# Attention score matmuls of one decoder layer: two heads of 64 rows side by side in three passes, in place of one head of 128 stacked rows in two

## The chip, the core and the metric

The kernel runs on one core of one Trainium2 chip. A core has five engines that run their own instruction lists and meet only through semaphores: TensorE (PE in the profile; its weight loads have a row of their own, PEld), VectorE (DVE), ScalarE (ACT), GpSimd (POOL) and SyncE (SP), which here only starts DMAs. Matmul results land in PSUM (8 banks of 128 partitions by 512 fp32 numbers); everything else lives in SBUF, also 128 partitions. The metric is device time of one execution in microseconds (us).

## The reference

One decoder layer over x of shape (4, 512, 512): an attention block with memory slots, a cross attention, a gated FFN, each followed by a residual sum and a layer norm. The change touches the first block alone. For each batch b and each of 16 heads (64 query/key columns, 64 slots, 128 value columns) that block computes

```
q, k, v, g, s = x@Wq, x@Wk, x@Wv, x@Wg, clip(x@Ws, -32, 32)
z  = cumlogsumexp(s, time)            # running normaliser of the slots
hk = hk * exp(z[t-1] - z[t]) + k[t] (outer) exp(s[t] - z[t])
pv = softmax(q[t] @ hk)               # 64 slots
hv = hv * exp(z[t-1] - z[t]) + exp(s[t] - z[t]) (outer) v[t]
o[t] = pv @ hv
out = (rmsnorm(o) * gnorm * silu(g)) @ Wo
```

The two recurrences are computed as causal attention: with E = exp(s) and 1/Z its running sum, the first is causal(q k^T) @ E / Z, the second causal((softmax / Z) E^T) @ v. So each step needs two score products of the same form: a 64-row "left" operand (k, later E) against a 64-row "right" operand (q, later w = pv/Z), 512 by 512 with the lower half left out.

## The kernel before

**Precision.** TensorE takes fp32r operands in one pass, which keeps only the high part of an fp32 number. Each operand is therefore split into `hi` (the fp32r rounding, a cast on ACT) and `lo` (what is left, a subtraction on DVE), and a product is hi·hi + hi·lo + lo·hi. `mm3` (L61 to L66) issues the three passes for projections with 128 contraction rows.

**Scores before.** A head's score has only 64 contraction rows, half of the 128 of the array. `left[:, h]` therefore stacks the hi half and the lo half of the left operand of head h over 128 partitions, and `right_hi[:, h]`, `right_lo[:, h]` hold the right operand twice, on both halves. One pass with `right_hi` gives hi·hi + lo·hi, one with `right_lo` gives hi·lo + lo·lo: two passes (L469, L471) a head and key block.

**Work of a step.** The attention block is 32 steps (8 pairs of heads by 4 batches), numbered n. The first pair and the last are unrolled, the six between run as a hardware loop of 4 steps. Two heads of one pair share each step: their projected operands lie on partitions 0 to 63 and 64 to 127, as the projections leave them in PSUM (`HALF`). PE's order in a step is written by hand (`step`, L525):

1. `chunks(n, 0)`: scores of k and q; then the S projection of the next step
2. `slots`: causal scores times E, L499, 64 output partitions a head; then transposes, projections and the output projection of the step before
3. `chunks(n, 1)`: scores of E and w; then the Q and K projections of the next step
4. transposes of E, then `values` (L515)

**One call of `chunks`** goes through three chunks c: key block 0 (512 columns, banks `ch[0]`, `ch[1]` for the two heads), key block 1 (384 columns, banks `okb`, `tb`), key blocks 3 and 2 (256 columns each, banks `ch` again). Since c = 2 writes the banks that c = 0 wrote, PE waits ahead of c = 2 on `chunk_act`: ACT must have copied chunk 0 out (`copy_chunk0`, L618), one copy a head. DVE copies and masks chunks 1 and 2 (L729), POOL masks the diagonal blocks of chunk 0 (L356) after ACT's copy. `slots` and `values` wait on all of these. There are 64 calls in all.

**ACT and DVE around it.** `high_right`/`low_right` and `high_left`/`low_left` prepare the operands: 4 and 4 instructions of 64 partitions for a right operand, 2 and 2 for a left one. Each step prepares two of each: E's left after the first call, w's right before the second call, the next step's q and k after it. ACT's list in a step starts with `copy_chunk0(n, 0)`, right behind the squares (L662) of the step before; POOL's list starts with the mask of chunk 0, right behind `factor` (L363 to L371), a chain of five small operations on the sums of those squares.

Of the kernel before, what the change touches and what calls it, by code (L numbers as in the profile page):

```python
# [125 lines left out]
def phase_attention(nc, x, Wq, Wk, Wv, Wg, Ws, Wo, gw, acc, ident, norm):  # L126
# [5 lines left out]
    with ExitStack() as ctx:  # L132
# [18 lines left out]
        left = sb("left", [P, 2, T], F32R)  # L151
        right_hi = sb("right_hi", [P, 2, T], F32R)
        right_lo = sb("right_lo", [P, 2, T], F32R)
# [263 lines left out]
        def _(pe):  # L417
# [12 lines left out]
            def project(m, i, b, pair):  # L430
# [3 lines left out]
                if i == S:  # L434
                    wait(pe, right_ready, 2 * m)
                    pe.wait_ge(s_ready, pair + 1)
                elif i == VG:
                    wait(pe, left_ready, 2 * m)
# [18 lines left out]
            def chunks(n, which):  # L457

                for c in range(3):
                    for h in range(2):  # L460
                        bank = (okb, tb)[h] if c == 1 else ch[h]

                        if c == 0:
                            wait(pe, chunk_dve, 8 * n + 4 * which - 1 + h)
                        elif c == 2:
                            pe.wait_ge(chunk_act, 4 * n + 2 * which + h + 1)
                        for i, col, first in CHUNKS[c]:
                            out = bank[:, col:col + T - first]
                            pe.matmul(out, left[:, h, i * P:(i + 1) * P], right_hi[:, h, first:T],  # L469
                                      start=True, stop=False)  # L470
                            mm = pe.matmul(out, left[:, h, i * P:(i + 1) * P], right_lo[:, h, first:T],  # L471
                                           start=False, stop=True)
                        mm.then_inc(chunk_done, 1)
# [51 lines left out]
            def step(n, p, j, first, last):  # L525
# [7 lines left out]
                pe.wait_ge(left_ready, 2 * (2 * n) + 2)  # L533
                pe.wait_ge(right_ready, 2 * (2 * n) + 2)
# [18 lines left out]
                pe.wait_ge(left_ready, 2 * (2 * n) + 4)  # L553
                pe.wait_ge(right_ready, 2 * (2 * n) + 4)
# [28 lines left out]
        def _(act):  # L583
# [5 lines left out]
            def high_left(src):  # L589
                for h in range(2):  # L590
                    nc.scalar.copy(left[HALF[h], h, :], src[HALF[h], :]).then_inc(left_hi_ready, 1)
# [39 lines left out]
            def step(n, p, j, first, last):  # L631
# [8 lines left out]
                act.wait_ge(chunk_done, 12 * n + 6)  # L640
                high_left(eT)
# [13 lines left out]
                act.wait_ge(chunk_done, 12 * n + 12)  # L655
# [22 lines left out]
        def _(dve):  # L678
# [7 lines left out]
            def low_left(src, turn):  # L686
                for h in range(2):
                    dve.wait_ge(left_hi_ready, 2 * turn + h + 1)
                    nc.vector.tensor_tensor(left[HALF[1 - h], h, :], src[HALF[h], :],
                                            left[HALF[h], h, :].bitcast(F32), ALU.subtract).then_inc(left_ready, 1)  # L690

            def low_right(src, turn):
                for h in range(2):
# [1037 lines left out]
```

## Time and profile before

| what | value |
|---|---|
| time, median of 3 runs | 2264.56 us (2264.44 to 2269.01) |
| profiled execution, first to last instruction (span) | 2263.2 us |
| mean granted TensorE clock | 0.981 |
| PE busy / PEld busy | 2153.7 us / 1632.5 us |
| DVE / ACT / POOL busy | 1565.8 / 989.7 / 550.8 us |
| last instruction of `values` in the attention block | begins at 1318.7 us |

The profile gives the span of its own execution and not what lies around it. The median stands 1.4 us above that span. A matmul in the trace is shown from its start to its modelled end, which overlaps the next one, so what one costs the stream is the distance between starts. Where "[0.26 <-POOL ...]" stands behind a row, the engine had shown nothing for that long, and the name says what ended it.

### The profile page before, as it was taken

How to read it: one execution, taken by the hardware profiler on the slowest of the kernel's cores; microseconds unless marked ns; L12 is line 12 of the kernel's file. 1: busy time of each engine (PE TensorE's matmuls, PEld its weight loads, DVE VectorE, ACT ScalarE, POOL GpSimd, SP SyncE). 2: the span in 40 equal slices, each digit the busy share in tenths (PEclk: the TensorE clock that was granted, in tenths of full speed). 3: DMA queues.
4: the chain of work that ended last, by engine and by line, in shares of the span. 5: the costliest groups of instructions: out<-in, count | busy, mean ns of one | idle time of the engine just before them, and what ended most of it. 6: DMA issues, size and time to landing. Idle time of an engine off the chain costs nothing. (4 is left out here: it accounts for less than half of the span.)

```text
span 2263.2 us, 32522 instructions
## 1 busy us (share of the span) xinstructions
PE 2153.7 (95%) x11316; PEld 1632.5 (72%) x11316; DVE 1565.8 (69%) x2455; ACT 989.7 (44%) x2026; POOL 550.8 (24%) x632
## 2 busy tenths in 40 slices
PE   7999999999999999999999968999999979999996
PEld 6788878888787888878888754555555458778784
DVE  4776767767677676767768868888888645455557
ACT  2443443434344443444434324777777742111211
POOL 3142251232243142232422231221211011111111
PEclk9999999999999999999999978999999989999998
DMA  4000100101001001001000000000000010000001
GB/s 149 1 1 10 33 10 1 33 10 34 1 10 34 1 11 33 1 10 33 1 10 1 1 10 7 14 14 14 14 13 8 2 28 28 15 28 14 28 14 74
DMA packets 56039, 42.60 MB, mean 19 GB/s; under 512 B 13936, under 2 KB 46704, under 8 KB 55920
## 3 DMA queue, kind: packets, MB, share of 16 engines
q1 hardware_dynamic: 55920, 40.92, 5.9%
q8 instruction: 87, 1.43, 0.3%
q14 instruction: 32, 0.26, 0.0%
HBM read 32.78 MB, written 4.19 MB: 16 GB/s over the span
## 5 line engine op out<-in xcount | busy, mean ns | idle before, releaser
L1263 DVE TENSOR_REDUCE x_nm<-x_ps 128x1 f32<-128x512 f32 x512 | 342.3, 688 | 70.8 <-PE x_ps L1070 65.0
L1240 ACT ACTIVATE x_prob<-x_ps 128x1024 f32<-128x1024 f32 x256 | 261.7, 1027 | 115.7 <-PE x_ps L1088 115.0
L1070 PE MATMUL x_ps<-x_ks,x_qs 128*128 128x512 f32 x512 | 230.2, 456 | 7.7 <-DVE x_nm L1263 6.2
L356 POOL TENSOR_TENSOR a_causal<-a_causal,a_mask 128x128 f32<-128x128 f32 x128 | 68.4, 545 | 594.6 <-ACT a_causal L618 593.1
L64 PE MATMUL a_ps<-a_vg_hi,a_xT_lo 128*128 128x512 f32 x512 | 209.8, 410 | 1.9 <-DVE a_vg_lo L810 1.9
L65 PE MATMUL a_ps<-a_vg_lo,a_xT_hi 128*128 128x512 f32 x512 | 200.9, 392 | 0.0
L66 PE MATMUL a_ps<-a_vg_hi,a_xT_hi 128*128 128x512 f32 x512 | 200.9, 392 | 0.0
L1070 PEld LDWEIGHTS x_ps<-x_ks,x_qs 128*128 128x128 f32 x512 | 98.1, 192 | 133.2 <-DVE x_nm L1263 90.9
L469 PE MATMUL a_ps<-a_right_hi,a_left 128*128 128x256 f32 (+2 forms) x512 | 166.4, 341 | 20.1 <-issue 15.0
L596 ACT CAST a_right_hi<-a_og 64x512 fp32r<-64x512 f32 x128 | 79.2, 619 | 194.0 <-DVE a_og L784 191.7
L1088 PE MATMUL x_ps<-x_qs,x_ks 128*128 128x512 f32 x512 | 162.4, 400 | 0.0
L471 PE MATMUL a_ps<-a_right_lo,a_left 128*128 128x256 f32 (+2 forms) x512 | 158.9, 329 | 0.0
L64 PE MATMUL a_ps<-a_xT_hi,a_qks_lo 128*128 128x512 f32 x384 | 151.3, 394 | 2.8 <-DVE a_xT_lo L682 2.1
L65 PE MATMUL a_ps<-a_xT_lo,a_qks_hi 128*128 128x512 f32 x384 | 151.1, 394 | 0.0
L66 PE MATMUL a_ps<-a_xT_hi,a_qks_hi 128*128 128x512 f32 x384 | 150.5, 392 | 0.0
L515 PE MATMUL a_ps<-a_v,a_causal 128*128 128x128 f32 x1280 | 148.2, 275 | 0.7 <-POOL a_causal L356 0.7
L515 PEld LDWEIGHTS a_ps<-a_v,a_causal 128*128 128x128 f32 x1280 | 145.4, 192 | 0.9 <-POOL a_causal L356 0.9
L64 PE MATMUL f_ps<-f_xT_hi,f_gu_lo 128*128 128x512 f32 x352 | 140.0, 398 | 0.0
L65 PE MATMUL f_ps<-f_xT_lo,f_gu_hi 128*128 128x512 f32 x352 | 138.6, 394 | 0.0
L66 PE MATMUL f_ps<-f_xT_hi,f_gu_hi 128*128 128x512 f32 x352 | 138.2, 393 | 0.0
L1102 PE MATMUL x_ps<-x_prob,x_cv 128*32 128x512 f32 x1024 | 136.4, 605 | 0.6 <-ACT x_prob L1240 0.6
L729 DVE TENSOR_TENSOR a_causal<-a_ps,a_mask 128x384 f32<-128x384 f32 x256 | 125.0, 549 | 14.4 <-PE a_ps L471 13.6
(160 smaller groups left out, 4650.5 us busy)
## 6 DMA issues: line engine op xcount, KB each, us to landing
a_raw_vg<-in_L_attn_Wv_dram SPq DMA_DIRECT2D x8, 512.0 KB, 4.1
a_raw_vg<-in_L_attn_Wg_dram SPq DMA_DIRECT2D x8, 512.0 KB, 6.3
a_raw_qks<-in_L_attn_Wo_dram SPq DMA_DIRECT2D x8, 512.0 KB, 3.5
out_dram<-acc SPq DMA_DIRECT2D x8, 512.0 KB, 3.3
x_xrows<-acc SPq DMA_DIRECT2D x13, 256.0 KB, 2.8
acc<-in_x_dram SPq DMA_DIRECT2D x3, 1024.0 KB, 9.5
f_raw_down<-in_L_ffn_down_w_dram SPq DMA_DIRECT2D x11, 256.0 KB, 2.9
f_raw_gu<-in_L_ffn_gate_w_dram SPq DMA_DIRECT2D x11, 256.0 KB, 3.0
```

Source lines behind the costliest of these rows:

```text
L64: pe.matmul(out, w_lo, x_hi, start=start, stop=False)
L65: pe.matmul(out, w_hi, x_lo, start=False, stop=False)
L66: return pe.matmul(out, w_hi, x_hi, start=False, stop=stop)
L469: pe.matmul(out, left[:, h, i * P:(i + 1) * P], right_hi[:, h, first:T], start=True, stop=False)
L471: mm = pe.matmul(out, left[:, h, i * P:(i + 1) * P], right_lo[:, h, first:T], start=False, stop=True)
L515: mm = pe.matmul(ob[t // 2][:, c:c + P], causal[:, h, at:at + P], v[:, j % 2, i, h * DV:(h + 1) * DV], start=(i == 0), stop=(i == t))
L729: nc.vector.tensor_tensor(causal[:, h, CHUNK_AT[c]:CHUNK_AT[c] + CHUNK_LEN[c]], bank[:, 0:CHUNK_LEN[c]], m.rearrange("p a t -> p (a t)"), ...
L1070: pe.matmul(max_bank(u, i, par), qs[:, q, tile, st * P:(st + 1) * P], ks[:, q, tile // 2, par, :], start=True, stop=True).then_inc(max_don ...
L1088: mm = pe.matmul(exb[s % 2][:, par, :], ks[:, q, g, par, t * P:(t + 1) * P], qs[:, q, 2 * g + pair, :], start=True, stop=True)
L1102: mm = pe.matmul(avb[32 * i:32 * (i + 1), :], cv[:, q, t, g, :], prob[:, (s + i // 2) % 4, i % 2, :], start=(t == 0), stop=(t == TT - 1))
L1240: nc.scalar.activation(prob[:, s % 4, :, :], exb[s % 2], ACT.Exp, scale=X_SCALE)\
L1263: nc.vector.tensor_reduce(nm[:, q % 2, i % 4, par, i // 4:i // 4 + 1], max_bank(u, i, par), AX.X, ALU.max, negate=True).then_inc(max_read, 1)
```

## The change

The operands keep the layout in which the projections lie in PSUM: head 0 on partitions 0 to 63, head 1 on partitions 64 to 127. Nothing is stacked or doubled. `left_hi`, `left_lo`, `right_hi`, `right_lo` are each one tile of 128 by 512, made by one instruction of 128 partitions. A score is now three passes of 64 rows a head (lo·hi, hi·lo, hi·hi), and the two heads alternate pass by pass. Head 0's matmuls are placed in rows 0 to 63 of the array and head 1's in rows 64 to 127, and their outputs go to two different banks. PE signals `chunk_done` once a chunk instead of once a head, and waits for both heads' copies ahead of chunk 2. The left operand's lo part is computed for the two heads at once, and lo·lo is no longer in the sum.

```
@@ chunks (PE)
-                    for h in range(2):
-                        bank = (okb, tb)[h] if c == 1 else ch[h]
-
-                        if c == 0:
-                            wait(pe, chunk_dve, 8 * n + 4 * which - 1 + h)
-                        elif c == 2:
-                            pe.wait_ge(chunk_act, 4 * n + 2 * which + h + 1)
-                        for i, col, first in CHUNKS[c]:
-                            out = bank[:, col:col + T - first]
-                            pe.matmul(out, left[:, h, i * P:(i + 1) * P], right_hi[:, h, first:T],
-                                      start=True, stop=False)
-                            mm = pe.matmul(out, left[:, h, i * P:(i + 1) * P], right_lo[:, h, first:T],
-                                           start=False, stop=True)
-                        mm.then_inc(chunk_done, 1)
+                    banks = (okb, tb) if c == 1 else ch
+
+                    if c == 0:
+                        wait(pe, chunk_dve, 8 * n + 4 * which)
+                    elif c == 2:
+                        pe.wait_ge(chunk_act, 4 * n + 2 * which + 2)
+                    for i, col, first in CHUNKS[c]:
+                        for k, q in ((left_lo, right_hi), (left_hi, right_lo), (left_hi, right_hi)):
+                            for h in range(2):
+                                mm = pe.matmul(banks[h][:, col:col + T - first], k[HALF[h], i * P:(i + 1) * P],
+                                               q[HALF[h], first:T], start=k is left_lo,
+                                               stop=k is left_hi and q is right_hi)
+                    mm.then_inc(chunk_done, 1)
...
@@ ACT
             def high_right(src):
-                for h in range(2):
-                    for half in (h, 1 - h):
-                        nc.scalar.copy(right_hi[HALF[half], h, :], src[HALF[h], :]).then_inc(right_hi_ready, 1)
+                nc.scalar.copy(right_hi[:, :], src).then_inc(right_hi_ready, 1)
...
             def copy_chunk0(n, which):
                 for h in range(2):
-                    wait(act, chunk_done, 12 * n + 6 * which + h + 1)
+                    wait(act, chunk_done, 6 * n + 3 * which + 1)
                     nc.scalar.copy(causal[:, h, 0:CHUNK_LEN[0]], ch[h]).then_inc(chunk_act, 1)
...
@@ DVE
             def low_right(src, turn):
-                for h in range(2):
-
-                    dve.wait_ge(right_hi_ready, 4 * turn + 2 * h + 2)
-                    for half in (h, 1 - h):
-                        low = nc.vector.tensor_tensor(right_lo[HALF[half], h, :], src[HALF[h], :],
-                                                      right_hi[HALF[h], h, :].bitcast(F32), ALU.subtract)
-                    low.then_inc(right_ready, 1)
+                dve.wait_ge(right_hi_ready, turn + 1)
+                nc.vector.tensor_tensor(right_lo[:, :], src, right_hi[:, :].bitcast(F32), ALU.subtract)\
+                    .then_inc(right_ready, 1)
```

`high_left` and `low_left` change in the same way (2 instructions to 1), and the counts of all waits on `left_ready`, `right_ready` and `chunk_done` follow.

PE's list at the second call of `chunks` in a step, before (operands are named right first, then left; the shape is that of the output):

```order
L469 MATMUL a_ps<-a_right_hi,a_left 128x384
L471 MATMUL a_ps<-a_right_lo,a_left 128x384
L469 MATMUL a_ps<-a_right_hi,a_left 128x256 [waits a_chunk_act]
L471 MATMUL a_ps<-a_right_lo,a_left 128x256
L469 MATMUL a_ps<-a_right_hi,a_left 128x256
L471 MATMUL a_ps<-a_right_lo,a_left 128x256
L469 MATMUL a_ps<-a_right_hi,a_left 128x256 [waits a_chunk_act]
L471 MATMUL a_ps<-a_right_lo,a_left 128x256
```

The same place in the changed kernel, where "x2" is one matmul of each head:

```order
L470 MATMUL a_ps<-a_right_hi,a_left_lo 128x512
L470 MATMUL a_ps<-a_right_lo,a_left_hi 128x512 x2
L470 MATMUL a_ps<-a_right_hi,a_left_hi 128x512 x2
L470 MATMUL a_ps<-a_right_hi,a_left_lo 128x384 x2
L470 MATMUL a_ps<-a_right_lo,a_left_hi 128x384 x2
L470 MATMUL a_ps<-a_right_hi,a_left_hi 128x384 x2
L470 MATMUL a_ps<-a_right_hi,a_left_lo 128x256 [waits a_chunk_act]
```

A call has 24 matmuls where it had 16, and one wait on `chunk_act` (both copies) where it had two, one ahead of each head's part of chunk 2.

DVE's list around the first call of a step, before: the gated products of the step before, the four masked chunks, E's left operand, the clip of the next S.

```order
L804 TENSOR_TENSOR a_og<-a_ps,a_gate 128x512 [waits a_sq_done] x2
L729 TENSOR_TENSOR a_causal<-a_ps,a_mask 128x384 [waits a_chunk_done] x4
L689 TENSOR_TENSOR a_left<-a_eT,a_left 64x512 [waits a_left_hi_ready] x2
L703 TENSOR_SCALAR a_eT<-a_ps 128x512 [waits a_proj_done,a_left_ready]
```

And in the changed kernel:

```order
L796 TENSOR_TENSOR a_og<-a_ps,a_gate 128x512 [waits a_sq_done] x2
L721 TENSOR_TENSOR a_causal<-a_ps,a_mask 128x384 [waits a_chunk_done] x4
L685 TENSOR_TENSOR a_left_lo<-a_eT,a_left_hi 128x512 [waits a_left_hi_ready]
L695 TENSOR_SCALAR a_eT<-a_ps 128x512 [waits a_proj_done,a_left_ready]
```

Nothing changes its place on DVE or ACT. The groups of operand instructions are shorter.

## Rows read from the trace of the kernel before

**Rows 1.** Page, part 1: busy us, share of the span, instructions.
```profile
PE 2153.7 (95%) x11316; PEld 1632.5 (72%) x11316; DVE 1565.8 (69%) x2455; ACT 989.7 (44%) x2026; POOL 550.8 (24%) x632
```

**Rows 2.** Timeline, PE, second call of step 14: start us, us, what [idle before].
```profile
629.29 0.42 PE L469 MATMUL a_ps<-a_right_hi,a_left 128*128 128x512 f32 x1
629.55 0.39 PE L471 MATMUL a_ps<-a_right_lo,a_left 128*128 128x512 f32 x1
629.78 0.39 PE L469 MATMUL a_ps<-a_right_hi,a_left 128*128 128x512 f32 x1
...
630.24 0.33 PE L469 MATMUL a_ps<-a_right_hi,a_left 128*128 128x384 f32 x1
...
630.94 0.28 PE L469 MATMUL a_ps<-a_right_hi,a_left 128*128 128x256 f32 x1
631.06 0.28 PE L471 MATMUL a_ps<-a_right_lo,a_left 128*128 128x256 f32 x1
...
631.89 0.40 PE L64 MATMUL a_ps<-a_xT_hi,a_qks_lo 128*128 128x512 f32 x1
```

**Rows 3.** Timeline, ACT, the chunk 0 copies of that call.
```profile
630.03 1.09 ACT L618 COPY a_causal<-a_ps 128x512 f32<-128x512 f32 x2
```

**Rows 4.** Groups by line and form: busy us, mean ns | idle before.
```profile
L499 PE MATMUL a_ps<-a_causal,a_e 128*64 128x512 f32 x128 | 34.5, 617 | 8.0 <-POOL a_causal L356 5.8 <-DVE a_causal L729 2.2
L515 PE MATMUL a_ps<-a_v,a_causal 128*128 128x128 f32 x1280 | 148.2, 275 | 0.7 <-POOL a_causal L356 0.7
L618 ACT COPY a_causal<-a_ps 128x512 f32<-128x512 f32 x128 | 69.7, 607 | 12.8 <-PE a_ps L471 12.8
```

**Rows 5.** Timeline, PEld, loads of two column halves in slots.
```profile
609.20 0.15 PEld L499 LDWEIGHTS a_ps<-a_causal,a_e 128*64 128x64 f32 x2 [0.28 <-issue]
```

**Rows 6.** Timeline, PE, step 8: into slots without a wait.
```profile
689.10 0.39 PE L66 MATMUL a_ps<-a_xT_hi,a_qks_hi 128*128 128x512 f32 x1
689.42 2.37 PE L499 MATMUL a_ps<-a_causal,a_e 128*64 128x512 f32 x16
```

**Rows 7.** Timeline, PE, step 14: out of slots.
```profile
610.81 0.28 PE L499 MATMUL a_ps<-a_causal,a_e 128*64 128x128 f32 x2
611.03 1.09 PE L420 MATMUL a_ps<-ident,a_og 128*128 128x128 f32 x8
```

**Rows 8.** Timeline, PE, first call of step 14 and what follows.
```profile
602.52 0.48 PE L469 MATMUL a_ps<-a_right_hi,a_left 128*128 128x512 f32 x1
...
604.47 0.39 PE L469 MATMUL a_ps<-a_right_hi,a_left 128*128 128x256 f32 x1
604.69 0.28 PE L471 MATMUL a_ps<-a_right_lo,a_left 128*128 128x256 f32 x1
...
605.54 0.40 PE L64 MATMUL a_ps<-a_xT_hi,a_qks_lo 128*128 128x512 f32 x1
...
608.72 2.37 PE L499 MATMUL a_ps<-a_causal,a_e 128*64 128x512 f32 x16 [0.26 <-POOL a_causal L356]
```

**Rows 9.** Timeline, ACT and POOL, beside that call.
```profile
603.81 1.09 ACT L618 COPY a_causal<-a_ps 128x512 f32<-128x512 f32 x2
607.26 1.32 POOL L356 TENSOR_TENSOR a_causal<-a_causal,a_mask 128x128 f32<-128x128 f32 x2
```

**Rows 10.** Timeline, PE and DVE: waits for operands at both ends of the block.
```profile
42.12 0.47 PE L469 MATMUL a_ps<-a_right_hi,a_left 128*128 128x512 f32 x1 [2.44 <-DVE a_left L689]
67.76 0.47 PE L469 MATMUL a_ps<-a_right_hi,a_left 128*128 128x512 f32 x1 [0.95 <-issue]
1244.33 0.50 PE L469 MATMUL a_ps<-a_right_hi,a_left 128*128 128x512 f32 x1 [0.41 <-DVE a_left L689]
1273.98 0.50 PE L64 MATMUL a_ps<-a_xT_hi,a_qks_lo 128*128 128x512 f32 x1 [0.35 <-DVE a_gate L708]
1306.22 2.80 DVE L697 TENSOR_TENSOR a_right_lo<-a_og,a_right_hi 64x512 fp32r<-64x512 f32 x4 [1.28 <-ACT a_right_hi L596]
1309.12 0.77 PE L469 MATMUL a_ps<-a_right_hi,a_left 128*128 128x512 f32 x1 [5.19 <-issue]
```

More of the change, by code:

```diff
@@ L150, in phase_attention @@
         wo_lo = sb("wo_lo", [P, 2, D], F32R)
-        left = sb("left", [P, 2, T], F32R)
-        right_hi = sb("right_hi", [P, 2, T], F32R)
-        right_lo = sb("right_lo", [P, 2, T], F32R)
+        left_hi = sb("left_hi", [P, T], F32R)
+        left_lo = sb("left_lo", [P, T], F32R)
+        right_hi = sb("right_hi", [P, T], F32R)
+        right_lo = sb("right_lo", [P, T], F32R)
         eT = sb("eT", [P, T])
@@ L434, in project @@
                 if i == S:
-                    wait(pe, right_ready, 2 * m)
+                    wait(pe, right_ready, 2 * m - 1)
                     pe.wait_ge(s_ready, pair + 1)
                 elif i == VG:
-                    wait(pe, left_ready, 2 * m)
+                    wait(pe, left_ready, 2 * m - 1)
                     pe.wait_ge(vg_ready, pair + 1)
@@ L531, in next_project @@
                             project(n + 1, i, b1, pair1)
-                pe.wait_ge(left_ready, 2 * (2 * n) + 2)
-                pe.wait_ge(right_ready, 2 * (2 * n) + 2)
+                pe.wait_ge(left_ready, 2 * n + 1)
+                pe.wait_ge(right_ready, 2 * n + 1)
                 pe.wait_ge(e_ready, n + 1)
@@ L552, in step @@
                 next_project(VG + 2, VG + 3)
-                pe.wait_ge(left_ready, 2 * (2 * n) + 4)
-                pe.wait_ge(right_ready, 2 * (2 * n) + 4)
+                pe.wait_ge(left_ready, 2 * n + 2)
+                pe.wait_ge(right_ready, 2 * n + 2)
                 if at(n, 0) or at(n, 1):
@@ L589, in high_left @@
             def high_left(src):
-                for h in range(2):
-                    nc.scalar.copy(left[HALF[h], h, :], src[HALF[h], :]).then_inc(left_hi_ready, 1)
+                nc.scalar.copy(left_hi[:, :], src).then_inc(left_hi_ready, 1)
             def high_right(src):
-                for h in range(2):
-                    for half in (h, 1 - h):
-                        nc.scalar.copy(right_hi[HALF[half], h, :], src[HALF[h], :]).then_inc(right_hi_ready, 1)
+                nc.scalar.copy(right_hi[:, :], src).then_inc(right_hi_ready, 1)
             def copy_proj(m, i, b):
@@ L639, in step @@
                 copy_chunk0(n, 0)
-                act.wait_ge(chunk_done, 12 * n + 6)
-                high_left(eT)
+                act.wait_ge(chunk_done, 6 * n + 3)
+                high_left(eT[:, :])
                 next_proj(S)
@@ L654, in step @@
                 copy_chunk0(n, 1)
-                act.wait_ge(chunk_done, 12 * n + 12)
+                act.wait_ge(chunk_done, 6 * n + 6)
                 next_proj(Q, K)
@@ L686, in low_left @@
             def low_left(src, turn):
[L687 to L690, printed above, removed]
+                dve.wait_ge(left_hi_ready, turn + 1)
+                nc.vector.tensor_tensor(left_lo[:, :], src, left_hi[:, :].bitcast(F32), ALU.subtract)\
+                    .then_inc(left_ready, 1)
             def low_right(src, turn):
-                for h in range(2):
-                    dve.wait_ge(right_hi_ready, 4 * turn + 2 * h + 2)
-                    for half in (h, 1 - h):
-                        low = nc.vector.tensor_tensor(right_lo[HALF[half], h, :], src[HALF[h], :],
-                                                      right_hi[HALF[h], h, :].bitcast(F32), ALU.subtract)
-                    low.then_inc(right_ready, 1)
+                dve.wait_ge(right_hi_ready, turn + 1)
+                nc.vector.tensor_tensor(right_lo[:, :], src, right_hi[:, :].bitcast(F32), ALU.subtract)\
+                    .then_inc(right_ready, 1)
             def clip(m, b):
@@ L725, in mask_chunks @@
                     for h in range(2):
-                        dve.wait_ge(chunk_done, 12 * n + 6 * which + 2 * c + h + 1)
+                        dve.wait_ge(chunk_done, 6 * n + 3 * which + c + 1)
                         m = mask[:, 2:5, :] if c == 1 else mask[:, 0:3, :]
@@ L755, in step @@
                 mask_chunks(n, 0)
-                low_left(eT, 2 * n + 1)
+                low_left(eT[:, :], 2 * n + 1)
                 if not last:
-                    dve.wait_ge(left_ready, 4 * n + 4)
+                    dve.wait_ge(left_ready, 2 * n + 2)
                     clip(n + 1, b1)
```

## The prediction

> **What bounds the kernel now.** I read the page first: PE is busy 95% of the span, no other engine above 72% [rows 1]. Busy time of overlapping matmuls proves little, so I went to the timeline of PE and looked at the distances between starts. In the attention block they are even: a 512-column matmul starts 0.23 us after the one before, four of 384 columns take 0.70 (0.175 each), one of 256 takes 0.12 [rows 2]. Nearly every part of a step runs like that, end to end. So TensorE's stream is the bound there, and what DVE or ACT save is worth something only where PE shows an idle bracket. Such brackets are few and small in the steady steps: 0.26 us ahead of slots [rows 8], and they are larger in the first and the last steps [rows 10]. The cross attention and the FFN are not touched; I count them as unchanged.
>
> **One call as it stands.** The second call of a step takes from 629.29 to 631.89, so 2.60 us up to the first matmul of the Q projection [rows 2]. ACT starts its first copy of chunk 0 at 630.03 [rows 3], 0.48 after the last matmul of head 0's chunk 0 (629.55). The pair of copies takes 1.09 and one copy 0.607 [rows 3, 4], so the second starts 0.48 after the first. Before, head 0 goes out while head 1 is computed, and PE reaches chunk 2 after the copy is done: no stall.
>
> **Do the two heads overlap?** The trace has no matmul of 64 rows. It has the like for columns: slots runs two heads in the two column halves. 128 of its 512-column fp32 passes are busy 34.5 us, 0.27 each, while `values` pays 148.2/1280 = 0.116 for 128 columns, which is 0.46 for 512 [rows 4]. So two column halves run at once. Their weight loads overlap too: two loads fit in 0.15 us [rows 5]. Bounds for a pair of 64-row passes: from one pitch (0.23, 0.175, 0.12) to two. I take one pitch, since the slots rows are the nearest and the tiles there are as independent as here (own rows, own banks).
>
> **What it costs to change the array's division.** Into slots without a wait the distance is 689.42 - 689.10 = 0.32 against 0.23: +0.09. Out of it 611.03 - 610.81 = 0.22 against the 0.11 of its 128-column pairs: +0.1 [rows 6, 7]. Each call of `chunks` now has one such entry and one exit. Bounds: 0 and 0.3 a call; I take 0.2, of which 0.1 is the exit.
>
> **The new call, where ACT is free in time.** Entry 0.09. The third pair of chunk 0 starts 0.51 later (two pitches of 0.23 and 0.05 for a first load that is not hidden). Both heads finish together, so ACT's copies start at 0.51 + 0.48 = 0.99 and 1.47, and the second ends at 2.08. PE has finished issuing chunk 1 (three pairs of 0.175) at about 1.25 and now waits for both copies. It starts chunk 2 at 2.1, with an exposed first distance of 0.22 as in 604.47 to 604.69 [rows 8], then four of 0.12, and 0.12 + 0.1 to the exit: 2.1 + 0.22 + 0.48 + 0.22 = 3.0. With the entry 3.1, and 0.05 for the next load, it is 3.15 against 2.60: **+0.55 us**. So the matmuls save 0.65 us a call (three pitches for four), and 0.85 of waiting for ACT and 0.2 to 0.3 of switching eat it. Behind the waiting matmul stands the whole PE list (the Q and K projections), and everyone waits for those. This holds for the second calls of steps 0 to 30 (31) and for the first calls of seven steps in which ACT is through with its squares (the five entries of a loop iteration and the last two steps): 38 x 0.55 = +20.9 us.
>
> **The first call of the other 24 steps.** There ACT is busy with squares until 603.8 and its copies end at 603.81 + 1.09 = 604.90 [rows 9], 2.4 after the call's start at 602.52 [rows 8]. The new call starts chunk 2 there (2.43), and leaves at 2.43 + 0.22 + 0.48 + 0.22 = 3.35, against 605.54 - 602.52 = 3.02 now: +0.33. But slots begins at 608.72, and PE idled 0.26 ahead of it for POOL's mask, which ends at 607.26 + 1.32 = 608.58 and hangs on the squares, not on this call [rows 8, 9]. New: 3.35 + 12 x 0.23 + 0.09 = 6.20 after the start, the same 6.20 as now. So the stall covers the loss and nothing is gained: 0 a step (bounds -0.1 and +0.3; without that cover it would be 24 x 0.33 = +8).
>
> **ACT and DVE.** Each step loses 4 casts of a right operand to 1, twice, and 2 to 1 of a left, twice: 8 instructions on each engine. An instruction of 128 partitions costs what one of 64 does (copies 0.607 for 128x512; DVE's four take 2.80, 0.70 each [rows 4, 10]). DVE gets back 8 x 0.69 = 5.5 us a step, ACT about 4.5. In steady steps this is off the path. It pays where PE waits for operands [rows 10]: the start of step 0 (DVE's low chain is 4 + 2 instructions; ACT's K cast sets the pace, about -1.4), its second call (-0.95), two waits of 0.4 like the one at 1244.33 and two of 0.35 like the one at 1273.98 where DVE also does the norms (-1.5), and the last step's second call: PE starts at 1309.12, right after DVE's chain of 2.80 that began at 1306.22 having waited 1.28 for two casts; with one cast and one subtraction it starts about 2.8 earlier. Together -6.6; bounds -3 and -10.
>
> **Sum.** 20.9 + 0 - 6.6 = +14 us on the profiled span of 2263.2, whose median run reads 1.4 more: 2264.6 + 14 = **2279 us**.
>
> **Rival A: weight loads do not overlap between row halves.** For it: every pass loads 128 columns of weights, and `values` never gets below 0.116 us for a load with its matmul [rows 4]; the overlapping loads of rows 5 are of other columns, which may be why they overlap. Then each of the 24 passes takes 0.116: chunk 0 ends its last start at 0.68, ACT is done at 2.25, chunk 2 takes 0.1 + 11 x 0.116 + 0.22 more, with the entry 3.95: +1.35 x 38 = 51; the other 24 calls leave at 4.03 and reach slots at 6.88 instead of 6.20: 24 x 0.68 = 16. Sum 67 - 6.6 = +60: 2325 us. The Trainium skill, TensorE: Matmul & The Clock Gate, section on LDWEIGHTS, says that a load of 32 rows takes as long as one of 128, since columns count. It leaves open whether two halves load at once; no row of this case shows it.
>
> **Rival B: the halves do not overlap at all.** Then the passes cost 1.5 times the present: chunk 0 lasts 6 x 0.23, chunk 2 starts at 2.83 and lasts 12 x 0.12: 4.56 against 2.60, 38 x 1.96 = 74, and 24 x 1.1 = 27 in the others: +95, 2360 us. Against it: slots.
>
> **Rival C, the other side: the wait ahead of chunk 2 does not bite.** Its place is the same wait on both copies. If the copies were through when chunk 1 is issued (1.25 after the start), the call would take 0.09 + 1.25 + 0.1 + 0.6 + 0.22 = 2.25, so -0.35, 38 times -13, and with -6.6 the time is 2245. It turns at the point where the whole call is back at 2.6, so when chunk 2 may start at about 1.6. That asks for 1.1 us from the third pair to the end of the second copy; the rows give 0.48 + 0.48 + 0.61 = 1.57 [rows 2 to 4]. The Trainium skill, TensorEngine Tiling (Array Packing), section Theoretical Speedup, gives up to 2 times for 64 rows, which would make three passes cost 1.5 and bring this side; it looks at TensorE alone, and the price of this rival is from rows.
>
> **Rival D: about the same.** The division of the array costs nothing here (the exit and entry are hidden, -0.2 x 38 = -7.6) and the ends of the block give the full 10: +20.9 - 7.6 - 10 = +3, 2268. The rows on slots speak against a free switch.
>
> **Chances.** Forecast (2271 to 2288, from a switch of 0.1 to 0.3 a call and the bounds of the 24 covered calls and of the ends) 0.61; A 0.15; B 0.05; C 0.06; D 0.13. Faster or slower is told from no change at 0.2%, 4.5 us: C is faster; D splits, 0.09 same, 0.03 slower, 0.01 faster; the rest is slower, 0.84 with D's share. Range with 8 in 10: leaving out B and C and a little of D and A gives 2265 to 2328; the forecast's own stands above.
>
> **What would show it.** In the profile after: the starts of two heads' 64-row matmuls a few ns apart and pairs 0.23, 0.175, 0.12 apart (right), or 0.116 between all of them (A), or full pitches (B). A bracket of about 0.85 us ahead of the first 256-column pair, ended by ACT's copy L615, in the second calls; a call of about 3.1. Slots of the 24 steps still 6.2 after the call's start, with almost no bracket left for POOL. Distances of 0.32 and 0.22 at the entry and exit. Busy time of DVE lower by about 32 x 5.5 = 175 us. If chunk 2 starts within 1.6 us of a second call's start, the forecast is wrong on the side of faster; if calls take over 3.5, on the other.

## The result, and the profile after

| | before | after |
|---|---|---|
| time, median | 2265.31 us (2264.44 to 2269.01, 4 runs) | 2288.85 us (2282.64 to 2294.57, 4 runs) |
| ratio, 95% interval | | 1.0103, 1.0084 to 1.0122 |
| span / granted clock of the profiled run | 2263.2 us / 0.981 | 2285.8 us / 0.981 |
| last matmul of `values` begins | 1318.7 us | 1340.6 us |

The change costs 23.5 us. Of the 22.6 us between the spans, 21.9 are there when the attention block ends, so what follows it is nearly unchanged (0.7 us). The other engines were relieved. On the page after, DVE is at 1380.6 us where it was at 1565.8, ACT at 838.0 for 989.7 [rows 1]. Part 1 and one line of part 5:

```profile
PE 2143.3 (94%) x11828; PEld 1595.9 (70%) x11828; DVE 1380.6 (60%) x2199; ACT 838.0 (37%) x1770; POOL 539.8 (24%) x632
...
L470 PE MATMUL a_ps<-a_right_hi,a_left_lo 64*128 64x256 f32 (+2 forms) x512 | 97.2, 376 | 58.2 <-ACT a_causal L615 43.8
```

The idle time in the second line is new. The summary of PE's waits has it on top:

```profile
PE a_ps L470 <- ACT a_causal L615: 43.8, 64, 0.8
```

One wait for each of the 64 calls. The timeline of PE has the second call of step 14, which answers to [rows 2], then that step's first call with slots, which answers to [rows 6, 8]; "x2" is one matmul of each head:

```profile
614.34 0.50 PE L470 MATMUL a_ps<-a_right_hi,a_left_lo 64*128 64x512 f32 x2
...
616.61 0.39 PE L470 MATMUL a_ps<-a_right_hi,a_left_lo 64*128 64x256 f32 x2 [0.77 <-ACT a_causal L615]
...
620.45 2.38 PE L499 MATMUL a_ps<-a_causal,a_e 128*64 128x512 f32 x16
...
640.84 0.39 PE L66 MATMUL a_ps<-a_vg_hi,a_xT_hi 128*128 128x512 f32 x1
641.15 0.50 PE L470 MATMUL a_ps<-a_right_hi,a_left_lo 64*128 64x512 f32 x2
641.49 0.40 PE L470 MATMUL a_ps<-a_right_lo,a_left_hi 64*128 64x512 f32 x2
641.72 0.40 PE L470 MATMUL a_ps<-a_right_hi,a_left_hi 64*128 64x512 f32 x2
...
642.31 0.34 PE L470 MATMUL a_ps<-a_right_hi,a_left_hi 64*128 64x384 f32 x2
643.29 0.39 PE L470 MATMUL a_ps<-a_right_hi,a_left_lo 64*128 64x256 f32 x2 [0.63 <-ACT a_causal L615]
643.51 0.28 PE L470 MATMUL a_ps<-a_right_lo,a_left_hi 64*128 64x256 f32 x2
...
643.99 0.28 PE L470 MATMUL a_ps<-a_right_hi,a_left_hi 64*128 64x256 f32 x2
644.20 0.50 PE L64 MATMUL a_ps<-a_xT_hi,a_qks_lo 128*128 128x512 f32 x1
644.53 0.40 PE L65 MATMUL a_ps<-a_xT_lo,a_qks_hi 128*128 128x512 f32 x1
```

And ACT's timeline of that call, which answers to [rows 3]:

```profile
642.16 1.07 ACT L615 COPY a_causal<-a_ps 128x512 f32<-128x512 f32 x2 [0.24 <-PE a_ps L470]
```

Read the starts. Two heads share one pitch: 0.23 from pair to pair (641.49 to 641.72). ACT starts at 642.16, which is 0.44 after the last pair of chunk 0, and its two copies end at 643.23 (642.16 + 1.07). PE had started its last chunk 1 pair at 642.31 and begins chunk 2 at 643.29, 2.14 after the call's start. The call takes 644.20 - 641.15 = 3.05 us up to the Q projection, against 2.60.

### The profile page after: what moved, and what is told of

Its sections match the earlier page's. It is cut to its first block and busy times, and to the rows that moved or that the text cites. A ratio compares the mean times of both kernels' runs of the same rounds, so it can differ in the third digit from the quotient of the medians.

```text
span 2285.8 us, 32764 instructions
## 1 busy us (share of the span) xinstructions
PE 2143.3 (94%) x11828; PEld 1595.9 (70%) x11828; DVE 1380.6 (60%) x2199; ACT 838.0 (37%) x1770; POOL 539.8 (24%) x632
## 5 line engine op out<-in xcount | busy, mean ns | idle before, releaser
L700 DVE SCALAR_TENSOR_TENSOR a_gate<-a_gate,a_ps 128x256 f32<-128x256 f32 x128 | 53.9, 421 | 196.1 <-ACT a_gate L609 196.1
L721 DVE TENSOR_TENSOR a_causal<-a_ps,a_mask 128x384 f32<-128x384 f32 x256 | 130.4, 551 | 50.8 <-PE a_ps L470 50.8
L64 PE MATMUL a_ps<-a_xT_hi,a_qks_lo 128*128 128x512 f32 x384 | 157.4, 410 | 1.9 <-DVE a_xT_lo L679 1.9
L470 PE MATMUL a_ps<-a_right_hi,a_left_lo 64*128 64x256 f32 (+2 forms) x512 | 97.2, 376 | 58.2 <-ACT a_causal L615 43.8
L1440 POOL TENSOR_TENSOR f_h_lo<-f_h,f_h_hi 128x512 fp32r<-128x512 f32 x44 | 57.0, 1295 | 295.6 <-ACT f_h_hi L1574 295.6
```

The lines of the kernel that those rows point to most:

```text
L64: pe.matmul(out, w_lo, x_hi, start=start, stop=False)
L470: mm = pe.matmul(banks[h][:, col:col + T - first], k[HALF[h], i * P:(i + 1) * P], q[HALF[h], first:T], start=k is left_lo, stop=k is left_ ...
L721: nc.vector.tensor_tensor(causal[:, h, CHUNK_AT[c]:CHUNK_AT[c] + CHUNK_LEN[c]], bank[:, 0:CHUNK_LEN[c]], m.rearrange("p a t -> p (a t)"), ...
```

## The experiments

All times are medians; the runs of before beside them had medians of 2265.1 to 2265.7. Each experiment has one trace. A step is counted from its first call to the next step's first call. A "loop's edge" is the first call of a new loop iteration, in steps 8, 12, 16, 20 and 24. "Undisturbed" are the 16 steps among 2 to 27 that neither begin nor end at such an edge; what an undisturbed step takes is their mean.

One thing varies between the traces whatever the edit is: the matmul just ahead of the first call of step 0 starts anywhere from 37.6 to 41.1 us after the span's start (39.4 in before, 41.1 in the changed kernel). So a difference of 2 or 3 us between the ends of two blocks says nothing by itself.

**1. Chunk 0 in banks that chunk 2 does not write.** Then nothing in a call waits for ACT. The first call uses the two projection banks (`pj`), the second the two of `values` (`ob`); the S and VG projections wait for the copies instead.

```
+        def first_banks(b1, which):
+            return ob if which else [pj[b1 % 2], pj[(b1 + 1) % 2]]
...
-                    banks = (okb, tb) if c == 1 else ch
+                    banks = (first_banks(b1, which), (okb, tb), ch)[c]
...
-                    elif c == 2:
-                        pe.wait_ge(chunk_act, 4 * n + 2 * which + 2)
+                        if which:
+                            wait(pe, added, 4 * n)
```

> The changed kernel with the wait ahead of chunk 2 taken away by other banks: chunk 0 goes to the two projection banks in a step's first call and to the two output banks in its second, so chunk 2 overwrites nothing that ACT has still to copy (the S and VG projections wait for the copies instead). Theory (the wait of about 0.97 us for ACT's copies is what makes the change slower): no bracket inside a call, which takes 2.1 us to its exit instead of 3.05; all of that comes back in the second calls (31 x 0.9 = 28 us), in the first calls only until POOL's mask binds slots (about 5.55 after the call's start instead of 6.11, 31 x 0.55 = 17 us): 45 us less than the changed kernel, 2244, so about 20 less than the kernel before. Rival (the wait only stands in for another one just behind it): the S projection, slots or values start no earlier, under 10 us come back, about 2280. Rival (row halves do not really run at once): the matmuls themselves would be as late as in the kernel before and the time not below its 2265.

Measured: 2234.43 us (2231.44 to 2235.62), ratio to before 0.9864 (0.9849 to 0.9879). Timeline of PE, into slots in step 14 and the second call:

```profile
594.25 0.39 PE L66 MATMUL a_ps<-a_xT_hi,a_qks_hi 128*128 128x512 f32 x1
594.92 1.08 PE L504 MATMUL a_ps<-a_causal,a_e 128*64 128x512 f32 x4 [0.28 <-POOL a_causal L360]
...
615.58 0.49 PE L475 MATMUL a_ps<-a_right_hi,a_left_lo 64*128 64x512 f32 x2
...
616.74 0.34 PE L475 MATMUL a_ps<-a_right_hi,a_left_hi 64*128 64x384 f32 x2
616.92 0.28 PE L475 MATMUL a_ps<-a_right_hi,a_left_lo 64*128 64x256 f32 x2
617.04 0.28 PE L475 MATMUL a_ps<-a_right_lo,a_left_hi 64*128 64x256 f32 x2
...
617.72 0.50 PE L64 MATMUL a_ps<-a_xT_hi,a_qks_lo 128*128 128x512 f32 x1
```

Chunk 2 follows chunk 1 at the pitch of 0.18, and the call takes 2.14 us (617.72 - 615.58) instead of 3.05. An undisturbed step takes 38.86 where the changed kernel takes 40.42 (1.56 x 31 = 48). Its way from second to first call is shorter by 0.89, and that from first to second by 0.67, where the expectation had 0.9 and 0.55. Step 0 and the last step give 0.6 and 2.0 on top of their share. The theory came true and fell short: 54 us came back for the 45 expected, which had left out the ends. The wait is the whole loss and more: without it the row halves bring 1.36%. What PE waits for now is POOL's mask ahead of slots: 594.92 - 594.25 = 0.67, where the bare entry is 0.32.

**2. Before, with the joint wait alone.** PE's passes stay as they were; ACT's copies wait for both heads and chunk 2 for both copies.

```
-                            pe.wait_ge(chunk_act, 4 * n + 2 * which + h + 1)
+                            pe.wait_ge(chunk_act, 4 * n + 2 * which + 2)
...
-                    wait(act, chunk_done, 12 * n + 6 * which + h + 1)
+                    wait(act, chunk_done, 12 * n + 6 * which + 2)
```

> The kernel before with the signals and waits of the change alone: ACT copies chunk 0 only when both heads are done, PE waits for both copies ahead of either head's chunk 2; matmuls and operands stay as before, so no array is divided. Theory: the second copy ends about 2.3 after the call's start and the second call takes 3.4 instead of 2.6, 38 x 0.8 = 30 us; the other first calls lose 0.5, of which slots' bracket hides 0.26, 24 x 0.2 = 5: +35 us, 2300. Rival (the division of the array is what costs, not the wait): within 5 us of 2265.

Measured: 2294.31 us (2292.32 to 2295.81), ratio 1.0125 (1.0110 to 1.0141). Timeline of PE, second call of step 14:

```profile
644.06 0.45 PE L469 MATMUL a_ps<-a_right_hi,a_left 128*128 128x512 f32 x1
...
645.55 0.33 PE L471 MATMUL a_ps<-a_right_lo,a_left 128*128 128x384 f32 x1
646.35 0.39 PE L469 MATMUL a_ps<-a_right_hi,a_left 128*128 128x256 f32 x1 [0.47 <-ACT a_causal L618]
...
647.41 0.40 PE L64 MATMUL a_ps<-a_xT_hi,a_qks_lo 128*128 128x512 f32 x1
```

The theory came true: the wait by itself costs 1.25%, more than the whole change. The call takes 3.35 us, 0.75 over before. It is the hand-over of both heads at once that costs, not the 64-row passes.

**3. Head 0's passes ahead of head 1's.** The changed kernel with the loop over heads outside those over key blocks and passes.

```
-                    for i, col, first in CHUNKS[c]:
-                        for k, q in (...):
-                            for h in range(2):
+                    for h in range(2):
+                        for i, col, first in CHUNKS[c]:
+                            for k, q in (...):
```

> The changed kernel with the passes of head 0 ahead of those of head 1 in each chunk instead of alternating; the same matmuls, loads, tiles, signals and waits. Theory (two row halves run at once only when neighbours in the list are of different halves): starts 0.23, 0.175 and 0.12 apart throughout, 24 of them; chunk 0's copies end 2.8 after the start, a call leaves at 4.4 instead of 3.05: 38 x 1.35 + 24 x 1.1 = 77 us more than the changed kernel, 2366. Rival (the order does not matter, since a half that is free takes its next pass): as the changed kernel, 2289.

Measured: 2312.91 us (2305.98 to 2315.39), ratio 1.0212 (1.0197 to 1.0228). Neither expectation came true. The timeline of PE, second call of step 14, shows why:

```profile
606.68 0.50 PE L470 MATMUL a_ps<-a_right_hi,a_left_lo 64*128 64x512 f32 x2
607.01 0.40 PE L470 MATMUL a_ps<-a_right_lo,a_left_hi 64*128 64x512 f32 x2
...
608.83 0.39 PE L470 MATMUL a_ps<-a_right_hi,a_left_lo 64*128 64x256 f32 x1 [0.65 <-ACT a_causal L615]
...
609.17 0.28 PE L470 MATMUL a_ps<-a_right_hi,a_left_hi 64*128 64x256 f32 x1
609.18 0.39 PE L470 MATMUL a_ps<-a_right_hi,a_left_lo 64*128 64x256 f32 x2
609.40 0.28 PE L470 MATMUL a_ps<-a_right_lo,a_left_hi 64*128 64x256 f32 x2
...
609.88 0.28 PE L470 MATMUL a_ps<-a_right_hi,a_left_hi 64*128 64x256 f32 x1
610.08 0.50 PE L64 MATMUL a_ps<-a_xT_hi,a_qks_lo 128*128 128x512 f32 x1
```

In chunk 0 the order is now three passes of head 0, then three of head 1, and still the first row has both heads' first pass, 0.01 us apart. So head 1's first pass, fourth in the list, overtook two passes of head 0. Up to there it is as the rival said, a half that is free takes its next pass. In chunk 2 each head has six passes, and there it is not. The first three of head 0 start alone (608.83, 609.06, 609.17), then head 1's first, seventh in the list, starts at 609.18, and head 1's last three run alone at the end: 0.35 us more a call. Over 64 calls that is 22 us, against 24 between the medians and 18.5 between the spans. My theory had assumed that TensorE starts passes in the order of the list. The Trainium skill, TensorE: Matmul & The Clock Gate, Part 3: Packing small matmuls, says the same as that theory, that matmuls are strict FIFO in start and end; the starts in this trace do not agree with it for passes in different row halves.

**4 and 5. The relief of ACT and DVE taken back.** Experiment 4 adds to the changed kernel the casts and subtractions that the change removed, as spare ones ahead of the real ones. Experiment 5 splits and orders the operand instructions as before had them: two halves, each with a spare one beside it, of which the second half's signal counts.

```
 e4, low_right (high_right, high_left and low_left in the same way):
+                for g, h in ((0, 0), (0, 1), (1, 0)):
+                    nc.vector.tensor_tensor(spare_lo[HALF[h], g, :], src[HALF[h], :], ...)
                 nc.vector.tensor_tensor(right_lo[:, :], src, ...).then_inc(right_ready, 1)
 e5, low_right:
-                nc.vector.tensor_tensor(right_lo[:, :], src, ...).then_inc(right_ready, 1)
+                for h in range(2):
+                    dve.wait_ge(right_hi_ready, 2 * turn + h + 1)
+                    nc.vector.tensor_tensor(spare_lo[HALF[h], :], src[HALF[h], :], ...)
+                    low = nc.vector.tensor_tensor(right_lo[HALF[h], :], src[HALF[h], :], ...)
+                low.then_inc(right_ready, 1)
```

> The changed kernel with as many operand instructions on ACT and DVE as before: 3 more of 64 partitions ahead of each right operand, 1 more ahead of each left one, written to a spare tile that nobody reads. The extra results are not used. Theory (the relief of ACT and DVE is worth something only at the ends of the block, 6.6 us in my sum): steady steps keep their 40.4 us, first and last steps are longer, 5 to 8 us more than the changed kernel, 2296. Rival (ACT and DVE are near enough to the path in every step): over 0.3 us a step, 10 us or more on top of the ends, 2305 or more.

> The changed kernel with its operands made by as many instructions, in the same order and with the same signals as in the kernel before: halves of 64 partitions, and for the right operand a second copy of each half into a spare tile that nobody reads. The earlier run with spare instructions put them all ahead of the real one and so made the chain to the second call longer than it was in the kernel before; this one does not. Theory (ACT's and DVE's relief is off the path in steady steps, since in the kernel before w's low part was ready 0.3 us before PE wanted it): steady steps keep 40.4 us, only the ends grow, 5 us more than the changed kernel, 2294. Rival (the relief is needed in every step, as that run seemed to say): 0.5 us a step or more, 2305 or more.

Measured: experiment 4 2322.89 us (2319.57 to 2329.61), ratio 1.0259 (1.0241 to 1.0278); experiment 5 2290.72 us (2286.21 to 2294.41), ratio 1.0112 (1.0095 to 1.0129). In experiment 4 DVE began its chain only when all four of ACT's casts were through, and PE's second call waits for it. DVE's and PE's timeline:

```profile
612.63 2.08 DVE L698 TENSOR_TENSOR a_spare_lo<-a_og,a_right_hi 64x512 bf16<-64x512 f32 x3 [2.42 <-ACT a_right_hi L598]
```

```profile
614.31 0.39 PE L66 MATMUL a_ps<-a_vg_hi,a_xT_hi 128*128 128x512 f32 x1
615.41 0.50 PE L472 MATMUL a_ps<-a_right_hi,a_left_lo 64*128 64x512 f32 x2 [0.72 <-issue]
```

An undisturbed step takes 41.21 for 40.42, and the time is that of the rival (2305 or more), but for another reason than the rival's. This was a bad undoing, since it makes that chain longer than it was before the change, where casts and subtractions ran side by side. In the changed kernel w's low part ends 3.1 us ahead of the second call (638.07 for 641.15), and the added parts outlast that by 0.8. Experiment 5 is the true one. Its second call, on PE's timeline, is entered without a wait:

```profile
638.51 0.39 PE L66 MATMUL a_ps<-a_vg_hi,a_xT_hi 128*128 128x512 f32 x1
638.83 0.50 PE L472 MATMUL a_ps<-a_right_hi,a_left_lo 64*128 64x512 f32 x2
```

An undisturbed step takes what it takes in the changed kernel (40.43 for 40.42), as the theory said. The block ends 2.1 us later (1342.7 for 1340.6), but that is a chance sum: the trace comes to its first call earlier and has 5.0 us of falls of the clock at three loop's edges (experiments 9 and 10 show such falls), which the changed kernel's has not. The relief has to be read where it acts. The wait ahead of the first call is 2.08 for 1.01 (+1.07), step 0 takes 24.92 for 25.20 from first to second call (-0.28), and step 31 24.74 for 23.20 (+1.54). So the 177 us of DVE and 145 of ACT that experiment 5 puts back are worth about 2.3 us, all outside the undisturbed steps. The two ratios by themselves leave -4 to +8.

**6. Before with the banks of experiment 1.** The edit is that of experiment 1, in before's loop over heads.

> The kernel before (stacked operands, two passes of 128 rows, heads in turn) with chunk 0 in the projection and output banks and no wait ahead of chunk 2. It says how much of the gain of the version with other banks is the banks' own. Theory (the kernel before waits for no copy in its second calls, and in its first calls slots' wait for POOL takes back what the banks give): 0 to 3 us less than the kernel before, 2263. Rival (the banks themselves are worth most of the 31 us): 2240 or less.

Measured: 2267.35 us (2264.99 to 2269.14), ratio 1.0008 (0.9999 to 1.0017). Before never waited in the second calls, and in the first ones the time goes to POOL. The timeline of PE into slots, step 14:

```profile
607.49 0.39 PE L66 MATMUL a_ps<-a_xT_hi,a_qks_hi 128*128 128x512 f32 x1
608.52 2.37 PE L504 MATMUL a_ps<-a_causal,a_e 128*64 128x512 f32 x16 [0.64 <-POOL a_causal L359]
```

The bracket of 0.26 [rows 8] has become 0.64. The rival is gone: the banks alone bring nothing; with 64-row passes they bring 54 us.

**7 and 8. POOL's mask ahead of its chain.** `factor`, five small operations of which one takes 1.64 us, is moved behind the mask of chunk 0: in experiment 7 on top of experiment 1, in experiment 8 on before.

```
                 mask_diagonals(n, 0)
                 if not first:
+                    factor(n - 1)
                     scale_o(n)
...
-                factor(n)
```

> The version with other banks, and POOL masks chunk 0 of a step ahead of the five factor operations of the step before, which now stand behind the masks. In that version slots waits 0.35 us for POOL's mask in 24 or more steps. Theory (slots is held by POOL's chain of factor and mask there): slots begins about 0.35 us earlier, 5.1 after the first call's start, and 8 to 10 us are gained, 2225. Rival (scale_o comes later by as much and the transposes behind slots wait for it instead): no gain, 2234.

> The kernel before with the same new order on POOL alone. Theory (slots waits 0.26 us for POOL's mask in 24 steps): that bracket goes, 6 us less than the kernel before, 2259. Rival (the wait moves to the transposes behind slots or to another mask): 2265.

Measured: experiment 7 2234.09 us (2233.15 to 2234.51), ratio 0.9861 (0.9846 to 0.9876), the same as experiment 1, which is what the rival said; experiment 8 2260.26 us (2257.62 to 2264.32), ratio 0.9979 (0.9968 to 0.9989), faster by 0.2% as forecast. The timeline of PE in experiment 7, step 14:

```profile
593.75 0.39 PE L66 MATMUL a_ps<-a_xT_hi,a_qks_hi 128*128 128x512 f32 x1
594.06 2.37 PE L505 MATMUL a_ps<-a_causal,a_e 128*64 128x512 f32 x16
596.54 1.09 PE L425 MATMUL a_ps<-ident,a_og 128*128 128x128 f32 x8
```

Slots start at the bare entry of 0.31, 5.09 after the first call's start instead of 5.45. But `scale_o` now stands behind `factor` on POOL, and the transposes that wait for it are 0.17 later behind slots, so an undisturbed step takes 38.72 for 38.86, not 0.36 less. Most of that is lost again: the five steps behind a loop's edge take 39.1 each where four of them took 38.5 in experiment 1. Experiment 8 keeps more of what the edit gives: its undisturbed step takes 39.35 for 39.68.

**9 and 10. A projection between chunk 1 and chunk 2.** By then the one open point was the price of changing the array's division. Experiment 9 makes experiment 1 leave the 64-row division and come back once more a step, where nothing waits. Experiment 10 does the same to the changed kernel, where it also covers ACT's copies; its edit is shown.

```
                     mm.then_inc(chunk_done, 1)
+                    if c == 1 and between is not None:
+                        between(Q)
...
-                chunks(n, 1)
-                next_project(Q, K)
+                chunks(n, 1, next_project)
+                next_project(K)
```

> The kernel with chunk 0 in other banks (2234.4 us), and in the second call of a step the Q projection moved to between chunk 1 and chunk 2, so PE leaves the 64-row division and comes back once more per step. No wait is in the way there, so this prices the change of division by itself. Theory (the switch term of the prediction was too small): in the traces the exit costs 0.09, the entry 0.09, and the first distance behind each is 0.10 longer than the pitch. Distances around the moved projection: chunk 1 to Q 0.265, Q first to second 0.335, Q to chunk 2 0.32, chunk 2 first to second 0.22, chunk 2 to K 0.21, K first to second 0.335, sum 1.685, against 0.175 + 0.12 + 0.21 + 0.335 + 0.23 + 0.23 = 1.30 where it stands now. So +0.385 a step, 31 steps, +12 us: 2246 us. Rival 1, the prediction's size of 0.2 an entry with its exit: +6, 2240. Rival 2: a change of division is free where nothing is waited for and the 0.3 in the traces belong to the waits beside them: 2234. The masks of chunk 2 on DVE come 2.8 us later; if values had to wait for them, a gap ahead of values would show.

> The changed kernel (2289 us) with the same move: the Q projection stands between chunk 1 and chunk 2 of the second call, so that PE computes while ACT copies chunk 0. The banks are those of the changed kernel, chunk 2 still waits for both copies. Theory: the wait (0.80 us in each of 31 second calls) is gone, and one more entry and exit costs 0.385 less the 0.10 of the first distance behind the wait, which was there already. Distances now 0.98 + 0.22 + 0.21 + 0.335 + 0.23 + 0.23 = 2.205, then 0.265 + 0.335 + 0.32 + 0.22 + 0.21 + 0.335 = 1.685: -0.52 a step, -16 us: 2273 us, still above before (2265.7). Rival, if the switch costs only 0.2: -0.7 a step, 2267. Rival, if the wait is not on ACT's copies but something inside TensorE ahead of the 256-column passes: it stays, and the time is 2289 or more.

Measured: experiment 9 2253.78 us (2248.69 to 2256.18), ratio 0.9946 (0.9930 to 0.9962); experiment 10 2277.47 us (2273.07 to 2284.51), ratio 1.0048 (1.0032 to 1.0064). PE's timeline of experiment 9, second call of step 14:

```profile
425.01 0.34 PE L475 MATMUL a_ps<-a_right_hi,a_left_hi 64*128 64x384 f32 x2
425.28 0.50 PE L64 MATMUL a_ps<-a_xT_hi,a_qks_lo 128*128 128x512 f32 x1
425.61 0.39 PE L65 MATMUL a_ps<-a_xT_lo,a_qks_hi 128*128 128x512 f32 x1
...
427.90 0.39 PE L66 MATMUL a_ps<-a_xT_hi,a_qks_hi 128*128 128x512 f32 x1
428.22 0.39 PE L475 MATMUL a_ps<-a_right_hi,a_left_lo 64*128 64x256 f32 x2
428.45 0.28 PE L475 MATMUL a_ps<-a_right_lo,a_left_hi 64*128 64x256 f32 x2
```

The distances are 0.27 out, 0.33 behind it, 0.32 in, 0.23 behind it: those that were expected, within 0.01. An undisturbed step grows from 38.86 to 39.29, +0.43 for 0.385; in experiment 10 it shrinks from 40.42 to 39.94, -0.48 for -0.52. So one entry with one exit costs 0.4 us, and the wait of the changed kernel was on ACT's copies and not on something inside TensorE: with the same banks, work in its place takes it away. Both medians lie 4 to 8 us above what was expected all the same. In experiment 10's trace, of its slowest run, that is in the steps behind a loop's edge; experiment 9's has 1.5 us more there than experiment 1's, and the rest of its excess stays open. PE's timeline of experiment 10 at step 12, and below it the granted clock ("PEclk", the figure behind the bracket):

```profile
528.11 0.50 PE L470 MATMUL a_ps<-a_right_hi,a_left_lo 64*128 64x512 f32 x2 [2.02 <-issue]
...
530.61 0.42 PE L470 MATMUL a_ps<-a_right_lo,a_left_hi 64*128 64x256 f32 x2
```

```profile
528.00:530.00 2.00, 1.50 (x12) 0.86 0.03 8
530.00:534.00 4.00, 3.77 (x17) 0.50 0.02 4
```

PE idles for 2 us at the loop's edge, goes on, and then the clock falls from full to half (2.4 to 1.2 GHz): the 256-column pairs stand 0.22 apart (530.61, 530.83) instead of 0.12. That step takes 42.60 instead of 39.94. Every one of the five edges has such a fall in experiment 10's trace (the steps behind them take 0.8 to 2.8 us more), three have one in experiment 5's, two in experiment 9's, one in experiment 1's and in before's, none in the changed kernel's and in experiment 7's.

## Why the prediction was right, and what it sized wrongly

The forecast was +14 us, the spans differ by 22.6. The mechanism and its place were as forecast. The term of switching was too small, the relief at the ends was counted too high, and much of the rest differs from one execution to the next.

**The halves overlap: right.** Pairs stand 0.23, 0.175 and 0.12 apart. The loads overlap as well; PE's weight loads in the same call:

```profile
641.15 0.19 PEld L470 LDWEIGHTS a_ps<-a_right_hi,a_left_lo 64*128 64x128 f32 x2 [0.35 <-issue]
641.26 0.19 PEld L470 LDWEIGHTS a_ps<-a_right_lo,a_left_hi 64*128 64x128 f32 x2
```

Two loads of 128 columns, one for each head, start together and a next pair 0.11 later. Rivals A and B are gone by that, and rival D with the change of division that is not free.

**The wait ahead of chunk 2: right.** Chunk 2 starts 2.14 after the call's start for a forecast of 2.1, in the second calls and at the loop's edges (369.80: 2.14), and at 2.27 in the other first calls for a forecast of 2.43. Rival C needed 1.6. Experiments 1 and 2 show that this wait is the cause: with it alone before loses 29 us, without it the changed kernel gains 54. Experiment 10 shows it again by giving PE something else to do.

**The 24 covered calls: right.** Slots start 6.11 after the first call's start (620.45 - 614.34), for 6.20 forecast and measured before. From first to second call these 24 steps change by -0.05 to +0.12, on average by 0.01.

**The price of the division: the step that was mis-sized.** The prediction put 0.2 on an entry with its exit, and 0.05 on the next load behind each. It read the entry and the exit off the slots rows, +0.09 and +0.1 [rows 6, 7], and both were right (641.15 - 640.84 = 0.31; 644.20 - 643.99 = 0.21). The distance behind each is longer by twice what it had put there: 641.15 to 641.49 is 0.34 and 644.20 to 644.53 is 0.33, where the pitch is 0.23. The bare sum is 0.4, and experiment 9 measured 0.43. The first call of a step follows `values`, and there the distance is 0.20 where before's was 0.03. A second call with its way to the next first call has grown from 12.89 to 13.61: +0.72 for +0.55 forecast. Over the 24 such stretches away from the loop's edges that is 4 us. The Trainium skill, TensorEngine Tiling (Array Packing), Tiling Modes, says that a change of the mode drains TensorE. The trace is in line with that: about 0.09 us more at each change and 0.10 behind it.

**The loop's edges: the calls right, the idle time beside them no term of the change.** The first calls behind an edge were forecast at +0.55 and four of the five measured at +0.52 to +0.59 (in the fifth, before's own trace has a fall of the clock). But the idle time of PE ahead of them grew as well: from second to first call it is +0.92 to +1.04 there, 0.2 to 0.3 over the 0.72 elsewhere. From the timeline of PE at step 8:

```profile
369.80 0.51 PE L470 MATMUL a_ps<-a_right_hi,a_left_lo 64*128 64x512 f32 x2 [2.23 <-issue]
```

Before it read 1.74 there. That adds 1.2 us for five edges. It is not a price of the row halves: the distance from the last matmul of an iteration to the first of the next is 2.01 to 2.12 in before and 2.42 to 2.51 in the changed kernel, but also 2.17 to 2.50 in experiment 6 and 2.05 to 2.57 in experiment 2, which have before's matmuls, and 1.95 to 2.27 in experiment 5, which has the changed kernel's. It differs from trace to trace, and what sets it stays open.

**The ends: right in the waits, too much credit for the relief.** The second call of step 31 is preceded by 2.71 us without a start where it was 5.46, so 2.75 for 2.8 forecast, and the waits of steps 30 and 31 are gone. They are gone in experiment 5 too, and with the longer call alone (experiment 2) the way to these two first calls is 0.45 over the usual, where before had 1.2. So it is mostly the longer call that covers them, and not the relief. From first to second call step 31 is only 0.89 shorter (23.20 for 24.09), since the matmul ahead of the wait starts 20.49 us after the first call for 18.63. Of that 0.9 is slots, whose matmuls took 3.28 us for 2.37: the granted clock was 0.81 between 1312 and 1316 us, and 1.00 at that place in before. At the start the first call's wait fell from 2.44 to 1.01 as forecast, but the matmuls ahead of it ended 1.7 us later in this trace, a difference as there is between any two. By experiment 5 the whole relief is worth about 2.3 us, where the sum took 6.6.

**The sum.** 8.6 us lie between the forecast's +14 and the 22.6 of the spans. 4 are the price of the division. The edges (1.2), the start (1.7) and step 31 (1.3) belong to these two executions as far as the traces show, and so does the fall of the clock in before's trace at step 20, which hides 1.6. The rest stays open. The median of 2288.85 us lies 10 above the forecast of 2279 and just over the 2288 to which it reached.

## What to carry to other kernels

Ask of a merged signal what the first of its parts was hiding. Here one head's copy ran under the other head's passes; finishing both together saved 0.65 us of matmuls a call and exposed 0.8 us of copying. Row halves are worth their price (0.4 us for each entry with its exit) where a stretch of them is long and its outputs go where nobody has to be waited for: the best version here is the changed kernel with chunk 0 in other banks, 1.36% under before, while of the two edits alone one costs 1.0% and the other brings nothing.

## What the chip showed that I had not expected

- Passes of different row halves do not start in the order of the list: the fourth of a list started 0.01 us after the first, and the seventh of another 0.01 us after the third (experiment 3). With six passes a head that reach was not enough, and alternating heads was 0.35 us a call faster.
- Changing the division costs twice at each side: 0.09 us on the change and 0.10 on the distance behind it.
- After a 2 us idle stretch at a loop's edge the granted clock fell to half in some traces and not in others, for 0.8 to 2.8 us of lost time each. That may be a large part of the spread of 1.4 to 12 us between runs of one kernel, and the time at which the block comes to its first call, which differs by 3.5 us between the traces, another. I infer both from the single traces, since the other runs have none: experiment 7, with no fall in its trace, has the spread of 1.4 us, and the trace with five falls is that of experiment 10's slowest run.
